# Working out a group's slots behind the third stage's statistics instead of in front of the first weighing

## The chip, the cores and the metric

One Trainium2 chip, one core. The metric is the device time of one execution in microseconds. In what follows PE is TensorE, DVE is VectorE, ACT is ScalarE, POOL is GpSimd and SP is SyncE.

## What is computed

64 graphs of 256 nodes with 256 features pass through two layers. Each of the four blocks is added to its input, which is first layer-normalised. The first is an attention over the graph's edges, the second a Mamba-2 block, the third a sum over four edge relations, and the fourth a mixture of eight experts to which each token is routed by its largest probability.

```
x = x + gnn_attention(_layernorm(x), adj, W, a)
x = x + mamba2_block(_layernorm(x), W_in, conv_w, ..., W_out, W_lin, b_lin)
x = x + relational_gnn(_layernorm(x), adj, weight, bias)
x = x + moe_ffn(_layernorm(x), gate_w, gate_b, w1, b1, w2, b2)
```

The routing is what the change is about:

```
C = max(1, math.ceil(CAPACITY_FACTOR * T / E))
idx = jnp.argmax(probs, axis=-1)
pos = (jnp.cumsum(one_hot, axis=0) * one_hot).sum(-1).astype(jnp.int32) - 1
kept = pos < C
buf = jnp.zeros((E, C, D), dtype=h.dtype).at[idx, pos_safe].set(x, mode='drop')
```

A token's slot is its expert's first row plus its place among that expert's tokens. Tokens beyond the capacity are not served.

## The kernel before

The program has two parts. The first runs over the 64 graphs (called batches) and holds all but the experts; it ends near 2420 us. The second runs the experts over 71 tiles of 256 tokens. Only the first part is touched.

The first part is a software pipeline written out by hand. `rounds` calls a function `step(b1_, b2_, b3_, turn_)` on every engine. In one step batch b1_ is in the first stage (attention), b2_, the batch before it, in the second (Mamba), and b3_, the one before that, in the third (relations and gate). The steps of an engine are executed in the order in which they are written; between engines there are only semaphores. Two batches form a group of 512 tokens, GB = 2, so steps alternate. In those with `turn_[1] == 0` the group before is routed (`best_expert`, with `counts` at the step's end), in those with `turn_[1] == 1` its slots are worked out (`slots`). The loop body holds two steps, one of each kind; the first six and the last few steps stand unrolled.

The order on DVE in one step (names as in the program):

- statistics of x of batch b1_ (`deviation(0, ...)`), xn2, then the convolution's taps, dt and the running sums cs, cs3, then the attention scores e and their maxima;
- g and xdt (L1023, L1027). PE needs them for the first exponents (L1256);
- in steps with slots: `slots` (L941 to L952), ten instructions on 4 or 32 numbers in a partition. It makes `slot` and `tid`, which POOL scatters one step later (`place`), and `prk`, the tokens' shares, which SP stores (L431);
- `weigh(range(0, 2))` (L901): the first two pairs of heads, once ACT's exponentials are there (L655);
- rsum and x1 (L1038, L1052), the attention's result. PE's next product with xT (`attend`, L1220) writes into the same two banks and so waits for x1_ready. Then the statistics of x1, from which POOL makes rstd and shift and ACT makes xn1, which PE turns (L1206);
- the other weighings, y (L1063, L1068), the third stage's result `row` (L1075). ACT squares y, POOL adds the squares up (y2h L561, y2s L564), and PE sums y2s over partitions (L1451, out_made);
- in steps with slots: the statistics of `row` (`deviation(3, ...)`, its last instruction L877). In steps with routing `best_expert` stands here and these statistics come after the mean square;
- the mean square, `ve[4]` (L1085). It waits for out_made; POOL raises it to the power -1/2 (L492), DVE makes x2 from it (L1094) and x2's statistics. PE needs x2_ready before the second pair of projections into bank 4 of the next step.

PE's order in a step: projections (L1211, L1281), masks by xp (L1328), relations (L1227, in pieces), transposes, attention's transposes (L1384), the first exponents (L1256 to L1265), a piece of relations, the attention product (L1411), the second exponents, a piece of relations, `attend` (L1220), the diagonal product (L1429), the last relations, xn1's transposes (L1206), the output projection (L1444), y2s (L1451).

Of the kernel before, what the change touches and what calls it, by code (L numbers as in the profile page):

```python
# [20 lines left out]
def need(eng, sem, n):  # L21

    if isinstance(n, int) and n <= 0:
        return
    eng.wait_ge(sem, n)
# [24 lines left out]
def graph_mamba_moe(nc, io, out):  # L50
# [39 lines left out]
    with ctx:  # L90
# [256 lines left out]
        def is_first(b):  # L347

            return isinstance(b, int) and b == 0
# [44 lines left out]
        def to_route(turn_):  # L394

            if turn_ is None or turn_[1] != 0 or is_first(turn_[0]):
                return None
            return turn_[0] - 1

        def to_slot(turn_):  # L400

            if turn_ is None or turn_[1] != 1 or is_first(turn_[0]):
                return None
            return turn_[0] - 1
# [390 lines left out]
        def _(dve):  # L795
# [73 lines left out]
            def deviation(i, src, chain, b):  # L869

                for t in range(T):
                    ins = v.bn_stats(stats[i][:, t, :], src[:, t, 0:D])
                chain.link(dve, ins, b, carry)
                for t in range(T):
                    ins = v.bn_aggr(mv[i][:, t, :], stats[i][:, t, :])
                chain.link(dve, ins, b)
                v.tensor_scalar(ve[i][:], mv[i][:, :, 1], EPS, None, ALU.add).then_inc(var_ready[i], 1)  # L877
# [27 lines left out]
            def best_expert(g):  # L905

                lk = lambda ins: chr_.link(dve, ins, g)
                three = lambda a: a[:].unsqueeze(2).broadcast_to([P, GT, E])
                chr_.start()
                dve.wait_ge(lg_in, GB * g + GB)  # L910
                lk(v.tensor_reduce(lmax[:], lg[:], AX.X, ALU.max))
                v.tensor_tensor(lg2[:], lg[:], three(lmax), ALU.subtract).then_inc(lg_ready, 1)
                dve.wait_ge(ge_ready, g + 1)
                v.tensor_reduce(gsum[:], ge[:], AX.X, ALU.add)
                lk(v.tensor_reduce(gmax[:], ge[:], AX.X, ALU.max))
                v.reciprocal(grec[:], gsum[:])
                lk(v.tensor_tensor(eq[:], ge[:], three(gmax), ALU.is_equal))
                v.tensor_tensor(prb[:], gmax[:], grec[:], ALU.mult)

                lk(v.tensor_tensor(rv[:], eq[:], rev[:], ALU.mult))  # L920
                lk(v.tensor_reduce(rmax[:], rv[:], AX.X, ALU.max))
                need(dve, cum_made, g)
                v.tensor_tensor(ohb[:], rev[:], three(rmax), ALU.is_equal).then_inc(oh_ready, 1)
                v.tensor_tensor(oh[:], rev[:], three(rmax), ALU.is_equal)
                need(dve, ids_out, 16 * GT * g)
                lk(v.tensor_scalar(tokf[:], tokf[:], float(GB * N), None, ALU.add))
                v.tensor_copy(tid[:], tokf[:])
                v.tensor_scalar(tr1[:], tokf[:], float(SLOTS + SPARE + 1), None, ALU.add)
# [9 lines left out]
            def slots(g):  # L938

                lk = lambda ins: chr_.link(dve, ins, g)  # L940
                v.tensor_tensor(limo[:], lim[:], oh[:], ALU.mult)  # L941
                lk(v.tensor_tensor(cumo[:], cum[:], oh[:], ALU.mult))
                v.tensor_reduce(lm[:], limo[:], AX.X, ALU.add)
                lk(v.tensor_reduce(slot1[:], cumo[:], AX.X, ALU.add))

                v.tensor_tensor(kept[:], slot1[:], lm[:], ALU.is_le)
                lk(v.tensor_tensor(df[:], slot1[:], tr1[:], ALU.subtract))
                lk(v.tensor_tensor(kd[:], kept[:], df[:], ALU.mult))
                lk(v.scalar_tensor_tensor(df[:], kd[:], -1.0, tr1[:], ALU.add, ALU.add))
                v.tensor_copy(slot[:], df[:]).then_inc(slot_ready, 1)  # L950
                need(dve, prk_out, 16 * g)
                v.tensor_tensor(prk[:, :, 0], prb[:], kept[:], ALU.mult).then_inc(prk_ready, 1)  # L952
# [5 lines left out]
            def step(b1_, b2_, b3_, turn_):  # L958
# [62 lines left out]
                if b2_ is not None:  # L1021
# [3 lines left out]
                    for t in range(T):  # L1025
# [2 lines left out]
                                              bank[4 + t][:, :].rearrange("p (h c) -> p h c", h=H),  # L1028
                                              dtT[:, t, :].unsqueeze(2).broadcast_to([P, H, HD]), ALU.mult)
                        ins.then_inc(xdt_ready, 1)  # L1030
                g_ = to_slot(turn_)
                if g_ is not None:
                    slots(g_)
                if b2_ is not None:
                    weigh(range(0, 2), b2_)
                if b1_ is not None:
# [40 lines left out]
                g_ = to_route(turn_)  # L1077
                if g_ is not None:
                    best_expert(g_)
                elif b3_ is not None:  # L1080
                    dve.wait_ge(x3_ready, b3_ + 1)
                    deviation(3, row[:, :, 0:D], ch4, b3_)
                if b2_ is not None:
                    dve.wait_ge(out_made, b2_ + 1)
                    v.tensor_scalar(ve[4][:], bank[5][:, 0:T], 1.0 / DIN, EPS, ALU.mult, ALU.add).then_inc(var_ready[4], 1)  # L1085
# [21 lines left out]
                if g_ is not None:  # L1107
                    counts(g_)

            rounds(dve, step)  # L1110
            best_expert(GROUPS - 1)
            counts(GROUPS - 1)
# [439 lines left out]
```

## Time and profile before

| | us |
|---|---|
| median of three runs | 3455.23 |
| lowest, highest | 3453.88, 3458.61 |
| profiled execution | 3474.3 |
| its span | 3472.6 |

| engine | busy us | share of the span |
|---|---|---|
| PE | 3346.5 | 96% |
| DVE | 2531.6 | 73% |
| ACT | 1745.4 | 50% |
| POOL | 1842.6 | 53% |

The span is what the trace covers of the profiled execution; the time of that execution is 1.7 us longer. It is to be compared with the median only with its own distance of 19 us in mind. The granted clock of TensorE was 0.986 of its full 2.4 GHz on average.

How to read it: a timeline row has the start in us from the span's start, the time taken in us, the engine, the line, the operation, output<-inputs and the number of instructions merged into the row; in brackets stands the idle time in front of it and what ended it. Matmuls are pipelined, so the rows of PE overlap a little, and a wait shorter than the pipeline is deep shows as a longer row rather than as idle time. A list of waits names the waiting line, what it waited for, the total in us, the number of times and the longest.

### The profile page before, as it was taken

The numbers are of one execution on the slowest core, as the hardware profiler recorded it, in microseconds if no ns is written. First come the engines' busy times: TensorE is split into PE (matmuls) and PEld (weight loads), VectorE is DVE, ScalarE is ACT, GpSimd is POOL, SyncE is SP. The second block draws the span as 40 slices with busy tenths as digits, with TensorE's granted clock in tenths as the row PEclk, the third lists the DMA queues.
The fourth block names the chain that finished last, engine by engine and source line by source line (L and its number), as shares of the span: only waits on it lengthen the run. The fifth ranks groups of instructions, "written<-read, shape, count | busy, mean of one in ns | idle before, by whom it ended". The sixth has DMA issues, their size and how long they took to land.

```text
span 3472.6 us, 60750 instructions
## 1 busy us (share of the span) xinstructions
PE 3346.5 (96%) x18826; PEld 2741.4 (79%) x18826; DVE 2531.6 (73%) x7305; ACT 1745.4 (50%) x3434; POOL 1842.6 (53%) x2172
## 2 busy tenths in 40 slices
PE   7999999999999999999999999996899999999998
PEld 6777777777777777777777777775788888888887
DVE  4888888878888888888888888886344444444444
ACT  3666656655656656656566565663223333333222
POOL 3455555555555565555655556554445555555543
PEclk8999999999999999999999999998899999999999
DMA  3111111111111111111111111110555555555553
GB/s 125 41 38 52 40 46 46 37 37 52 40 39 49 40 40 52 37 46 45 37 52 40 46 46 37 52 37 22 174 195 191 192 195 198 197 192 193 193 194 129
DMA packets 168166, 304.66 MB, mean 88 GB/s; under 512 B 38000, under 2 KB 140400, under 8 KB 149936
## 3 DMA queue, kind: packets, MB, share of 16 engines
q0 software_dynamic: 38272, 196.98, 16.5%
q1 hardware_dynamic: 92880, 72.41, 7.3%
q10 hardware_dynamic: 36960, 34.62, 3.3%
q8 instruction: 26, 0.43, 0.1%
q14 instruction: 28, 0.23, 0.0%
HBM read 250.77 MB, written 53.17 MB: 88 GB/s over the span
## 4 chain that ended last, share of the span: by engine, by line
PE 92%; DVE 3%; issue 2%; POOL 1%; another core or an unknown queue 1%; ACT 1%; DMA 1%; SPq 0%; DVEq 0%; ACTq 0%; POOLq 0%
PE bank L1211 14%; PE bank L1485 14%; PE bank L1499 14%; PE bank L1227 13%; PE bank L1328 7%; PE bank L1444 6%; PE bank L1429 5%; PE bank L1220 4%; PE bank L1411 3%; PE bank L1359 2%; PE bank L1281 2%; DVE decay L901 1%; PE bank L1350 1%; PE bank L1451 1%; PE bank L1474 1%
## 5 line engine op out<-in xcount | busy, mean ns | idle before, releaser
L786 ACT ACTIVATE decay<-bank,w_up 128x256 f32<-128x256 f32 x568 | 269.0, 474 | 700.0 <-PE bank L1485 694.2
L1227 PE MATMUL bank<-w_rel,hT 128*128 128x264 f32 x2048 | 540.7, 397 | 0.0
L1211 PE MATMUL bank<-xn1T,w_in 128*128 128x256 f32 x2304 | 524.1, 382 | 2.9 <-ACT xn1T L637 0.8
L1485 PE MATMUL bank<-zs,w_up 128*128 128x256 f32 x2272 | 503.8, 380 | 0.6 <-ACT zs L637 0.6
L1499 PE MATMUL bank<-w_dn,decay 128*128 128x256 f32 x2272 | 502.1, 379 | 0.0
L1211 PEld LDWEIGHTS bank<-xn1T,w_in 128*128 128x128 f32 x2304 | 433.1, 190 | 61.0 <-issue 1.5
L1485 PEld LDWEIGHTS bank<-zs,w_up 128*128 128x128 f32 x2272 | 432.9, 191 | 60.1 <-issue 0.9
L1499 PEld LDWEIGHTS bank<-w_dn,decay 128*128 128x128 f32 x2272 | 426.2, 190 | 55.1
L1159 DVE TENSOR_TENSOR hT<-bank,w_dn 128x256 f32<-128x256 f32 x142 | 60.3, 425 | 535.9 <-PE bank L1499 535.9
L892 DVE SCALAR_TENSOR_TENSOR conv<-bank,conv_w,conv 128x255 f32<-128x255 f32 (+2 forms) x960 | 426.2, 477 | 20.8
L1227 PEld LDWEIGHTS bank<-w_rel,hT 128*128 128x128 f32 x2048 | 358.6, 190 | 85.7 <-issue 32.8
L506 POOL TENSOR_SCALAR masks<-adjt_sb 128x512 fp32r<-128x512 int32 x256 | 419.4, 1651 | 5.4
L492 POOL TENSOR_TENSOR rstd<-ve,mhalf 128x2 f32<-128x2 f32 x256 | 212.9, 831 | 284.0 <-DVE ve L877 239.5
L369 POOL TENSOR_TENSOR beats<-mhalf 128x1 f32<-128x1 f32 x372 | 100.1, 269 | 462.7 <-DVE hT L1159 335.9
L901 DVE SCALAR_TENSOR_TENSOR decay<-decay,g 128x768 f32<-128x768 f32 x256 | 266.5, 1081 | 60.2 <-ACT decay L655 57.3
L543 POOL TENSOR_TENSOR x2b<-x,b_rel 128x264 f32<-128x264 f32 x128 | 93.9, 753 | 397.6 <-DVE xdt L1027 389.9
L1328 PE MATMUL bank<-masks,xp 128*128 128x512 f32 x1024 | 275.7, 414 | 5.7 <-ACT xp L637 5.7
L655 ACT ACTIVATE decay<-bank 128x768 f32<-128x768 f32 x256 | 193.6, 808 | 144.7 <-PE bank L1265 115.6
L1328 PEld LDWEIGHTS bank<-masks,xp 128*128 128x128 f32 x1024 | 189.1, 190 | 68.3 <-ACT hT L637 25.1
L1444 PE MATMUL bank<-w_proj,y 128*128 128x264 f32 x1024 | 239.4, 387 | 0.7 <-DVE y L1068 0.7
L1444 PEld LDWEIGHTS bank<-w_proj,y 128*128 128x128 f32 x1024 | 189.2, 190 | 31.2 <-DVE y L1068 2.3
L591 POOL DMA_INDIRECT w_in<-token_rows,idc x142 | 178.9, 1260 | 43.6 <-issue 43.6
(258 smaller groups left out, 5997.0 us busy)
## 6 DMA issues: line engine op xcount, KB each, us to landing
token_rows<-row SPq DMA_DIRECT2D x64, 266.0 KB, 3.0
xT_sb<-in_xT ACTq DMA_DIRECT2D x64, 256.0 KB
x_sb<-in_x ACTq DMA_DIRECT2D x64, 256.0 KB, 3.0
adj_sb<-in_adj SPq DMA_DIRECT2D x64, 256.0 KB, 3.4
adjt_sb<-in_adjT SPq DMA_DIRECT2D x64, 256.0 KB, 3.5
out<-row SPq DMA_DIRECT2D x64, 256.0 KB, 2.4
w_in<-token_rows,idc POOLq DMA_INDIRECT x142
out<-hT,ids POOLq DMA_INDIRECT x142
```

What stands on the lines that cost most here:

```text
L492: gp.tensor_tensor(rstd[i][:], ve[i][:], mhalf[:], ALU.pow).then_inc(rstd_ready[i], 1)
L506: ins = gp.tensor_scalar(masks[:, :, r, :], adjt[:], float(r + 1), None, ALU.is_equal)
L655: nc.scalar.activation(decay[:, 2 * j:2 * j + 2, :], expo_banks[j % 2][:, :, 0:TRI], ACT.Exp).then_inc(decay_ready, 1)
L786: nc.scalar.activation(hid(f), bank[f % 4][:, 0:GROUP], ACT.Relu, bias=b1[q % 2][:, f:f + 1]).then_inc(hid_ready, 1)
L892: ins = v.scalar_tensor_tensor(conv[:, c, k:N], src[:, 0:N - k], conv_w[:, c, TAPS - 1 - k:TAPS - k], conv[:, c, k:N], ALU.mult, ALU.add)
L901: v.scalar_tensor_tensor(decay[:, 2 * j:2 * j + 2, :], decay[:, 2 * j:2 * j + 2, :], 1.0, g[:, 0:TRI].unsqueeze(1).broadcast_to([P, 2, TRI ...
L1211: ins = mm(dst, w_in[:, k, first:first + P], xn1T[:, k, :], start=k == 0, stop=k == DK - 1)
L1227: ins = mm(bank[6 + t][:, 0:GX], hT[:, d, r * N + t * P:r * N + (t + 1) * P], w_rel[:, r, d, :], start=r == 0 and d == 0, stop=r == R - 1 ...
L1328: ins = mm(bank[6 + c][:, :], xp[part][:, t, d * P:(d + 1) * P], masks[:, t, 2 * c:2 * c + 2, :], start=t == 0 and part == 0, stop=t == T ...
L1444: ins = mm(bank[(4, 2)[t]][:, 0:GX], y[:, j, t * P:(t + 1) * P], w_proj[:, j, :], start=j == 0, stop=j == XB - 1)
L1485: ins = mm(bank[f % 4][:, 0:GROUP], w1[i][:, k, f * P:(f + 1) * P], xgT[:, k, :], start=k == 0, stop=k == DK - 1)
L1499: ins = mm(bank[4 + j][:, 0:D], hid(f)[:, j * P:(j + 1) * P], w2[i][:, f, :], start=f == 0, stop=f == FB - 1)
```

## The change

The call of `slots` in a step that has one is moved. It stood behind xdt and in front of the first weighing. Now it stands behind the statistics of `row` and in front of the wait for out_made and the mean square. A step without a second stage (b2_ is None; only the very last one) keeps the call where it was, and so does the call after the last step. The variable for the group is renamed, since `g_` is set anew in between. 30 calls are moved, those for groups 0 to 29.

```diff
--- before.py
+++ after.py
@@ -1028,9 +1028,9 @@
                                               bank[4 + t][:, :].rearrange("p (h c) -> p h c", h=H),
                                               dtT[:, t, :].unsqueeze(2).broadcast_to([P, H, HD]), ALU.mult)
                         ins.then_inc(xdt_ready, 1)
-                g_ = to_slot(turn_)
-                if g_ is not None:
-                    slots(g_)
+                placed = to_slot(turn_)
+                if placed is not None and b2_ is None:
+                    slots(placed)
                 if b2_ is not None:
                     weigh(range(0, 2), b2_)
                 if b1_ is not None:
@@ -1080,6 +1080,8 @@
                 elif b3_ is not None:
                     dve.wait_ge(x3_ready, b3_ + 1)
                     deviation(3, row[:, :, 0:D], ch4, b3_)
+                if placed is not None and b2_ is not None:
+                    slots(placed)
                 if b2_ is not None:
                     dve.wait_ge(out_made, b2_ + 1)
                     v.tensor_scalar(ve[4][:], bank[5][:, 0:T], 1.0 / DIN, EPS, ALU.mult, ALU.add).then_inc(var_ready[4], 1)
```

DVE, an unrolled step with slots, around the old place, before. The names in it: `decay<-decay,g` is a weighing, `x<-bank,rsum,x_sb` is x1.

```order
L1027 TENSOR_TENSOR xdt<-bank,g 128x512 x2
L941 TENSOR_TENSOR limo<-lim,oh 128x32
L942 TENSOR_TENSOR cumo<-cum,oh 128x32
L943 TENSOR_REDUCE lm<-limo 128x4
L944 TENSOR_REDUCE slot<-cumo 128x4
L946 TENSOR_TENSOR kept<-slot,lm 128x4
L947 TENSOR_TENSOR df<-slot,tr 128x4
L948 TENSOR_TENSOR kd<-kept,df 128x4
L949 SCALAR_TENSOR_TENSOR df<-kd,tr 128x4
L950 CAST slot<-df 128x4
L952 TENSOR_TENSOR prk<-prb,kept 128x4
L901 SCALAR_TENSOR_TENSOR decay<-decay,g 128x768 x2
```

The same place in the change:

```order
L1027 TENSOR_TENSOR xdt<-bank,g 128x512 x2
L901 SCALAR_TENSOR_TENSOR decay<-decay,g 128x768 x2
L1038 RECIPROCAL rsum<-esum 128x2
L1052 SCALAR_TENSOR_TENSOR x<-bank,rsum,x_sb 128x264 x2
L872 BN_STATS stats<-x 128x6 x2
```

The weighing and x1 follow xdt directly.

DVE, the end of the same step, before. `row<-bank,x2b` is the third stage's result, `ve<-row` its variance, `ve<-bank` the mean square, `x<-bank,rstd,x1b` is x2.

```order
L1075 TENSOR_TENSOR row<-bank,x2b 128x2x264
L872 BN_STATS stats<-row 128x6 x2
L371 MEMSET beats 128x1
L875 BN_AGGR row<-stats 128x2 x2
L877 TENSOR_SCALAR ve<-row 128x2
L1085 TENSOR_SCALAR ve<-bank 128x2
L1094 SCALAR_TENSOR_TENSOR x<-bank,rstd,x1b 128x264 x2
```

The same place in the change:

```order
L877 TENSOR_SCALAR ve<-row 128x2
L941 TENSOR_TENSOR limo<-lim,oh 128x32
L942 TENSOR_TENSOR cumo<-cum,oh 128x32
L943 TENSOR_REDUCE lm<-limo 128x4
L944 TENSOR_REDUCE slot<-cumo 128x4
L946 TENSOR_TENSOR kept<-slot,lm 128x4
L947 TENSOR_TENSOR df<-slot,tr 128x4
L948 TENSOR_TENSOR kd<-kept,df 128x4
L949 SCALAR_TENSOR_TENSOR df<-kd,tr 128x4
L950 CAST slot<-df 128x4
L952 TENSOR_TENSOR prk<-prb,kept 128x4
L1087 TENSOR_SCALAR ve<-bank 128x2
```

The ten instructions stand between the variance and the mean square. The lines behind the edit have numbers two higher. In the loop body they stand in the same way. The instructions of PE, ACT, POOL and SP and their order are the same as before.

## Rows read from the trace of the kernel before

**Rows 1.** The page's chain that ended last, shares of the span by engine
```profile
PE 92%; DVE 3%; issue 2%; POOL 1%; another core or an unknown queue 1%; ACT 1%; DMA 1%; SPq 0%; DVEq 0%; ACTq 0%; POOLq 0%
```

**Rows 2.** Waits of TensorE's matmuls, 150 to 2350 us: total us, times, longest
```profile
PE bank L1220 <- DVE x L1052: 34.6, 33, 6.7
...
PE bank L1206 <- ACT xn L754: 2.0, 1, 2.0
```

**Rows 3.** Timeline of TensorE, step with slots: start us, us, engine line
```profile
1157.62 0.61 PE L1451 MATMUL bank<-ones_row,y2s 128*128 128x1 f32 x4
...
1178.65 0.58 PE L1256 MATMUL bank<-cs,sel 32*128 32x256 bf16 x4
...
1184.76 2.09 PE L1220 MATMUL bank<-w_gc,xT_sb 128*128 128x274 f32 x8 [0.91 <-DVE x L1052]
...
1194.63 0.61 PE L1451 MATMUL bank<-ones_row,y2s 128*128 128x1 f32 x4
```

**Rows 4.** Timeline of TensorE, the next step, without slots
```profile
1215.51 0.36 PE L1256 MATMUL bank<-cs,sel 32*128 32x256 bf16 x4
...
1220.32 2.02 PE L1220 MATMUL bank<-w_gc,xT_sb 128*128 128x274 f32 x8
...
1226.01 0.60 PE L1206 MATMUL bank<-identf,xn 128*128 128x128 f32 x4
...
1230.11 0.61 PE L1451 MATMUL bank<-ones_row,y2s 128*128 128x1 f32 x4
```

**Rows 5.** Timeline of DVE, step with slots, around the slots
```profile
1177.61 1.29 DVE L1027 TENSOR_TENSOR xdt<-bank,g 128x512 f32<-128x512 f32 x2
...
1178.81 0.18 DVE L941 TENSOR_TENSOR limo<-lim,oh 128x32 f32<-128x32 f32 x1
...
1181.26 0.15 DVE L952 TENSOR_TENSOR prk<-prb,kept 128x4 f32<-128x4 f32 x1
...
1183.72 0.89 DVE L1052 SCALAR_TENSOR_TENSOR x<-bank,rsum,x_sb 128x264 f32<-128x264 f32 x2
```

**Rows 6.** Timeline of DVE, step without slots, the first weighing
```profile
1216.95 2.07 DVE L901 SCALAR_TENSOR_TENSOR decay<-decay,g 128x768 f32<-128x768 f32 x2 [1.42 <-ACT decay L655]
```

**Rows 7.** Timeline of DVE, end of the step with slots
```profile
1193.18 0.62 DVE L877 TENSOR_SCALAR ve<-row 128x2 f32<-128x2 f32 x1
...
1195.27 0.16 DVE L1085 TENSOR_SCALAR ve<-bank 128x2 f32<-128x2 f32 x1 [1.47 <-PE bank L1451]
```

**Rows 8.** Timeline of POOL, step with slots: masks, y2s, power
```profile
1180.72 4.41 POOL L506 TENSOR_SCALAR masks<-adjt_sb 128x512 fp32r<-128x512 int32 x3
...
1193.85 0.72 POOL L564 TENSOR_TENSOR y2s<-y2h 128x256 f32<-128x256 f32 x1
...
1194.53 0.71 POOL L492 TENSOR_TENSOR row<-ve,mhalf 128x2 f32<-128x2 f32 x1
```

**Rows 9.** Timeline of all engines, slots of the last group
```profile
2422.23 0.18 DVE L941 TENSOR_TENSOR limo<-lim,oh 128x32 f32<-128x32 f32 x1
...
2423.61 0.16 DVE L952 TENSOR_TENSOR prk<-prb,kept 128x4 f32<-128x4 f32 x1
```

**Rows 10.** Timelines of POOL and DVE in the routing, end of a step
```profile
1156.81 0.76 POOL L564 TENSOR_TENSOR y2s<-y2h 128x256 f32<-128x256 f32 x1
...
1156.89 0.72 DVE L920 TENSOR_TENSOR rv<-eq,rev 128x32 f32<-128x32 f32 x1
```

**Rows 11.** Timeline of DVE, xn2 after a step with routing, then after one with slots
```profile
1163.45 0.73 DVE L882 TENSOR_SCALAR xn<-x,mv,rstd 128x256 f32<-128x256 f32 x2
...
1199.90 0.73 DVE L882 TENSOR_SCALAR xn<-x,mv,rstd 128x256 f32<-128x256 f32 x2
```

**Rows 12.** Timeline of ScalarE, step without slots, xn1
```profile
1224.77 1.09 ACT L754 ACTIVATE xn<-x,shift,rstd 128x256 f32<-128x256 f32 x2 [3.81 <-POOL shift L554]
```

**Rows 13.** Timelines of SP's queue and of POOL after the step with slots
```profile
1196.94 0.39 SPq L436 DMA_DIRECT2D adj_sb<-in_adj  x1
...
1205.08 1.94 POOL L530 TENSOR_SCALAR noedge<-adj_sb 128x512 f32<-128x512 int32 x1
```

## The prediction

> **What bounds the kernel now.** I read the chain that ended last first. TensorE carries 92% of it [rows 1], so an edit on VectorE (DVE) counts only where TensorE waits for DVE. The list of waits comes next: between 150 and 2350 us the largest total of matmul waits is L1220 on x1 (L1052), 34.6 us in 33 waits [rows 2]; 29 of them are alike, the other four are single stalls, the longest of 6.7 us. Then I laid two neighbouring steps side by side on TensorE. A step is counted from one L1451 (the mean square's sums) to the next. A step that works out slots (call it odd) lasts 1194.63 - 1157.62 = 37.01 us [rows 3]; the step without them (even) 1230.11 - 1194.63 = 35.48 us [rows 3, 4]. The DVE timeline of the same two steps shows why.
>
> **Where the odd step loses.** In the odd step L1256 starts at +21.03 and takes 0.58 us, in the even one at +20.88 and takes 0.36 [rows 3, 4]. So 0.15 + 0.22 = 0.37 us is lost up to the first exponents. That part isn't the slots': DVE enters the odd step later, because the routing (best_expert) stood in the tail before it. Its xn2 (L882) starts at 1163.45, that is +5.83, against +5.27 in the even step [rows 11]. L1220 then starts at +27.14 against +25.69, 1.45 later. Take off the 0.37 and 1.08 us is left. 0.91 of it is the marked wait for x1 [rows 3], the rest is pipeline filling. This part is the slots': xdt ends at 1178.90, slots run from 1178.81 until 1181.41 and x1 comes at 1183.72 [rows 5]. In the even step DVE has nothing there and idles 1.42 us until the exponentials are ready [rows 6]. Slots of 2.60 us in a gap of 1.42 push the weighing back by about 1.2.
>
> **What the change takes away.** Ten DVE instructions leave this place in 30 odd steps (groups 0 to 29). 29 of them have an L1220; the thirtieth, near the end, starts no next batch, and I put it at 0. Each of the 29 can gain at most the 1.08, which is all that sets it apart from an even step there. **Gain: 29 x 1.08 = 31 us.**
>
> **What it adds.** The same ten instructions now stand between the third stage's variance (L877, ends 1193.18 + 0.62 = 1193.80) and the mean square (L1085 in before), which waits for TensorE's L1451 and starts at 1195.27 after 1.47 us of idle time [rows 7]. The cover is thus 1.5 us. What the slots need there is not shown by the trace of before, so bounds: run with GpSimd (POOL) silent, in the last group, they take 2423.61 + 0.16 - 2422.23 = 1.54 us [rows 9]. At the old place they take 2.60, the last part of it beside POOL's masks [rows 5, 8]. At the new place POOL first does the y2s sum (1193.85 to 1194.57), then a power (1194.53 to 1195.24) [rows 8]. How such an addition holds up a small DVE instruction is seen in the routing: L920, two operands in SBUF, takes 0.72 us beside a y2s that began 0.08 us before it [rows 10], where limo, of the same size, takes 0.18 alone [rows 9]. I expect limo to slip in, cumo to be held until y2s ends (0.6 more) and perhaps kept to brush the power (0.1). So T = 1.54 + 0.65, about 2.2 us. It is nearer to the upper row because the same kinds of POOL work run beside it, but only one or two instructions can be caught, not three.
>
> The slots start about 1193.73 (instructions without a dependence start some 0.08 before the former one's recorded end). With T = 1.54 the mean square starts where it does now, with 2.2 about 0.6 later, with 2.6 about 1.0 later. Everything behind it on DVE moves by the same d: the power on POOL that waits for it, x2, its statistics, the next batch's statistics, xn2, the taps, dt, cs3, xdt. DVE has next to no idle time on that way in an even step.
>
> **What the delay costs on TensorE.** x2 itself has room: bank 4 is needed after the first two blocks of projections. The price is paid some 20 us later, where the first exponents need xdt. The trace gives the exchange rate: in the odd step DVE is 0.56 late at xn2 and TensorE loses 0.37 by the first exponents [rows 3, 4, 11]. So about 0.2 is absorbed and the rest is passed on in full. With d = 0.6 an even step loses 0.4, with 0 nothing, with 1.0 it loses 0.8. After that DVE waits for the exponentials anyway and is in step again, so losses don't pile up. 29 even steps follow a moved group and start from it. **Loss: 29 x 0.4 = 12 us** (0 to 23).
>
> **Small things.** limo and cumo may in turn hold y2s up. y2s ends at 1194.57 and L1451 starts at 1194.63 [rows 3, 8], so TensorE has no room there, and y2s later by up to 0.2 us makes L1451 as late. But this and the lateness of DVE run in parallel, and the larger of the two counts, so it adds nothing to 0.4. slot and tid are read by POOL's scatter only in the next step: no cost. On SP's queue the store of the shares (L431) now waits for a prk that comes around 1195.9 us; behind it is queued the load of adj, issued at 1196.94, which has to be there before noedge at 1205.08 [rows 13]. Even 1 us later there are 7 us left: cost 0. TensorE's, ScalarE's, POOL's and SP's own orders are unchanged.
>
> A rule of the Trainium skill bears on T. The row first: prk has two operands in SBUF, starts at 1181.26, takes 0.15 us, and the first mask on POOL has been running since 1180.72, about 1.5 us each [rows 5, 8]. It was not held. The page "SBUF — State Buffer", section "Who interferes with whom", says that a DVE instruction with two SBUF inputs contends with a GpSimd instruction that reads SBUF, and that the one that starts second is blocked until the first ends. By that rule kept would wait for the whole power too, T would be about 2.3, and the time 3 us more than my forecast. The row of prk speaks against a full block each time, the row of L920 for it.
>
> **The sum.** -31 + 12 = -19 us. The profiled execution took 3474.3 us (span 3472.6), 19 above the median of 3455.2; the steps of a kind agree within 0.1 us apart from a few with single stalls, so I take the same difference for both: 3474.3 becomes 3455, and the median becomes **3436 us**.
>
> **Rivals.**
> (a) The slots fit in the gap (T up to 1.8): nothing is passed on, all of the gain stays, 3424 us. For it: the idle time there is 1.47 us and the bare work 1.54. Against: y2s runs right there.
> (b) The slots stay as long as they were (2.6): loss 23, the sum -8, 3447 us. For it: POOL is busy here as well. Against: its work ends at 1195.24, and the last four instructions have DVE to themselves.
> (c) **Another wait takes the place of x1's**, and the kernel gets slower. In the even step the weighing collides with POOL's masks; they end later, and with them the shift that xn1 needs: xn1 is done at 1224.77 + 1.09 = 1225.86, and L1206 needs it at 1226.01 [rows 4, 12]. The odd step will run like that, with 0.15 us of room. Each microsecond beyond it is lost at L1206 in full. With T = 2.2 the turning point is 0.7 beyond the room; with the masks 1.2 us later than in the even steps the sum is -19 + 35 = +16, 3471 us. Against it: over 60 steps L1206 waited for xn1 once, 2.0 us [rows 2].
> (d) The gain doesn't come, because x1 is held by something else as well (exponentials, the attention product), and only part of the loss remains: between -5 and +5, 3455 us. Against it: x1 in even steps is early enough.
>
> **Chances.** Forecast (T 1.9 to 2.4, 3430 to 3443) 55%; (a) 15%; (b) 13%; (d) 8%; (c) 9%. A measurement of this kernel can tell about 0.2% (7 us) from no change. The forecast, (a) and most of (b) lie beyond that: faster 77%. Within it: (d) and a part of (b), 13%. Slower: (c) and a remainder, 10%. The range of 8 in 10 reaches from 3423 to 3452.
>
> **What would show it.** In after: no wait of L1220 for x1 in odd steps and an odd step of 35.9 to 36.1 us (right), or a wait at L1206 in it (c). Slots at the new place of 2.2 us with cumo at 0.7 and the idle time before the mean square gone. Even steps of 35.9 rather than 35.5, with L1256 stretched and the start of xn2 0.6 later. Even steps unchanged mean (a), 36.3 and more (b). The forecast is wrong altogether if odd steps don't fall below 36.5.

## The result

The changed kernel takes 3423.22 us (3420.38 to 3426.49, four runs), the kernel before in the same runs 3454.56. The ratio is 0.9908, with an interval of 0.9896 to 0.9921: 32 us or 0.92% faster. The forecast was 3436 in a range of 3423 to 3452, so the way was right and the gain too small by 12 us; the measured time lies on the lower edge of the range. It is what rival (a) gave, 3424.

The chain that ended last, from the page of after, shares of the span by engine [rows 1]:

```profile
PE 94%; DVE 2%; issue 2%; POOL 1%; DMA 1%; ACT 0%; another core or an unknown queue 0%; SPq 0%; ACTq 0%; DVEq 0%; POOLq 0%
```

Waits of TensorE's matmuls from 150 to 2350 us: total, times, longest. L1222 is L1220 of before, L1208 is L1206 [rows 2]:

```profile
PE bank L1208 <- ACT xn L754: 2.7, 2, 2.0
PE bank L1222 <- DVE x L1052: 1.6, 2, 1.2
```

34.6 us of waiting for x1 have become 1.6; the two left are single stalls in even steps.

TensorE in two neighbouring steps of after: a step with slots from 1197.74 on, the next without from 1233.72 on. L1453, L1258, L1222 and L1208 answer to L1451, L1256, L1220 and L1206 [rows 3, 4]:

```profile
1197.74 0.61 PE L1453 MATMUL bank<-ones_row,y2s 128*128 128x1 f32 x4
...
1218.77 0.58 PE L1258 MATMUL bank<-cs,sel 32*128 32x256 bf16 x4
...
1223.81 2.02 PE L1222 MATMUL bank<-w_gc,xT_sb 128*128 128x274 f32 x8
...
1229.50 0.60 PE L1208 MATMUL bank<-identf,xn 128*128 128x128 f32 x4
...
1233.72 0.51 PE L1453 MATMUL bank<-ones_row,y2s 128*128 128x1 f32 x4
...
1254.52 0.35 PE L1258 MATMUL bank<-cs,sel 32*128 32x256 bf16 x4
...
1259.33 2.02 PE L1222 MATMUL bank<-w_gc,xT_sb 128*128 128x274 f32 x8
...
1269.16 0.61 PE L1453 MATMUL bank<-ones_row,y2s 128*128 128x1 f32 x4
```

The step with slots lasts 35.98 us instead of 37.01. L1222 starts in it at +26.07, before at +27.14: this is the 1.08 of the prediction, all but 0.01 of it. The step without slots lasts 35.44 instead of 35.48. Nothing of the expected 0.4 is in it: L1258 starts at +20.80 and takes 0.35. A pair is 1.07 us shorter, and 29 of these are 31 us.

DVE in the same step with slots, around the old place and then at the new one [rows 5 to 7, 9]:

```profile
1217.73 1.29 DVE L1027 TENSOR_TENSOR xdt<-bank,g 128x512 f32<-128x512 f32 x2
1220.44 1.96 DVE L901 SCALAR_TENSOR_TENSOR decay<-decay,g 128x768 f32<-128x768 f32 x2 [1.42 <-ACT decay L655]
...
1222.55 0.89 DVE L1052 SCALAR_TENSOR_TENSOR x<-bank,rsum,x_sb 128x264 f32<-128x264 f32 x2
...
1232.61 0.17 DVE L877 TENSOR_SCALAR ve<-row 128x2 f32<-128x2 f32 x1
1232.69 0.18 DVE L941 TENSOR_TENSOR limo<-lim,oh 128x32 f32<-128x32 f32 x1
1232.79 0.18 DVE L942 TENSOR_TENSOR cumo<-cum,oh 128x32 f32<-128x32 f32 x1
...
1233.32 0.26 DVE L946 TENSOR_TENSOR kept<-slot,lm 128x4 f32<-128x4 f32 x1
...
1233.69 0.16 DVE L948 TENSOR_TENSOR kd<-kept,df 128x4 f32<-128x4 f32 x1
...
1234.19 0.17 DVE L952 TENSOR_TENSOR prk<-prb,kept 128x4 f32<-128x4 f32 x1
1234.27 0.15 DVE L1087 TENSOR_SCALAR ve<-bank 128x2 f32<-128x2 f32 x1
...
1238.89 0.73 DVE L882 TENSOR_SCALAR xn<-x,mv,rstd 128x256 f32<-128x256 f32 x2
```

POOL beside it [rows 8]:

```profile
1221.55 5.41 POOL L506 TENSOR_SCALAR masks<-adjt_sb 128x512 fp32r<-128x512 int32 x3
...
1232.82 0.74 POOL L564 TENSOR_TENSOR y2s<-y2h 128x256 f32<-128x256 f32 x1
1233.52 0.72 POOL L492 TENSOR_TENSOR row<-ve,mhalf 128x2 f32<-128x2 f32 x1
```

At the old place the weighing waits 1.42 us for the exponentials, as in a step without slots, and x1 starts at +24.81, before at +26.10. At the new place the ten instructions take 1234.19 + 0.17 - 1232.69 = 1.67 us, 0.13 above the bare 1.54 and far from the 2.2 of the forecast; in all 29 odd steps of after that start a next batch they take 1.63 to 1.68. That they fit where DVE idled 1.47 us comes from the overlap at both ends: limo begins 0.09 before the recorded end of L877, and the mean square 0.09 before that of prk. The mean square starts at +0.55 here. (After has two kinds of steps with slots. In this one, 18 of the 29, a mask held DVE's y up and the sums' row at 1233.72 takes 0.51; in the other kind it takes 0.61 and starts 0.10 earlier, the mean square is at +0.65, and the next step lasts 35.51.) Before it was at +0.64. xn2 starts at +5.17, before at +5.27: DVE enters the next step no later than it did. But the gap is full: DVE no longer idles before the mean square.

The thirtieth moved call, in the step that starts no next batch, ran much as the forecast had it for all: limo slipped in, cumo (2305.45) took 0.71 us and ended 0.05 after POOL's additions y2h (2304.68 to 2306.11), and the ten took 2.32 us. They also began 0.6 to 0.7 us earlier before the sums than elsewhere, so the mean square still stood at +0.64.

The profiled executions differ by 51 us in span (3472.6 and 3421.2), more than the runs do. The steps explain 31; the rest are single stalls that the trace of before happened to hold, one of 6.7 us at L1220 among them [rows 2]. That is why the medians, not the two profiled executions, give the size of the gain.

### The profile page after: what moved, and what is told of

It reads as the page before. It is cut to its first block, busy times and chain, and to the rows that moved or that the text cites. A ratio compares the mean times of both kernels' runs of the same rounds, so it can differ in the third digit from the quotient of the medians.

```text
span 3421.2 us, 60750 instructions
## 1 busy us (share of the span) xinstructions
PE 3333.2 (97%) x18826; PEld 2738.9 (80%) x18826; DVE 2506.8 (73%) x7305; ACT 1745.0 (51%) x3434; POOL 1871.5 (55%) x2172
## 4 chain that ended last, share of the span: by engine, by line
PE 94%; DVE 2%; issue 2%; POOL 1%; DMA 1%; ACT 0%; another core or an unknown queue 0%; SPq 0%; ACTq 0%; DVEq 0%; POOLq 0%
PE bank L1213 14%; PE bank L1487 14%; PE bank L1501 14%; PE bank L1229 14%; PE bank L1330 7%; PE bank L1446 6%; PE bank L1431 5%; PE bank L1222 3%; PE bank L1413 3%; PE bank L1361 2%; PE bank L1283 2%; PE bank L1352 1%; PE bank L1258 1%; PE bank L1476 1%; PE bank L1453 1%
## 5 line engine op out<-in xcount | busy, mean ns | idle before, releaser
L506 POOL TENSOR_SCALAR masks<-adjt_sb 128x512 fp32r<-128x512 int32 x256 | 456.4, 1795 | 5.4
L369 POOL TENSOR_TENSOR beats<-mhalf 128x1 f32<-128x1 f32 x372 | 121.6, 327 | 462.5 <-DVE hT L1161 336.1
L492 POOL TENSOR_TENSOR rstd<-ve,mhalf 128x2 f32<-128x2 f32 x256 | 190.5, 744 | 251.0 <-DVE ve L877 206.7
```

The lines of the kernel that those rows point to most:

```text
L492: gp.tensor_tensor(rstd[i][:], ve[i][:], mhalf[:], ALU.pow).then_inc(rstd_ready[i], 1)
L506: ins = gp.tensor_scalar(masks[:, :, r, :], adjt[:], float(r + 1), None, ALU.is_equal)
```

## The experiments

**How late may the mean square be?** The forecast's loss was a rate (all but 0.2 us is passed on) times a lateness. The filler is a statistics instruction on DVE whose result nobody reads; it touches only `row` and a tile of its own. It goes once behind and once ahead of the slots.

```diff
+            def filler(n):
+                for i in range(n):
+                    v.bn_stats(pad[:, i, :], row[:, i % T, 0:D])
...
                 if placed is not None and b2_ is not None:
                     slots(placed)
+                    filler(1)
```

> The changed kernel plus one bn_stats of 128x256 on DVE (0.37 us of start-to-start time, result unused) between the moved slots and the mean square, in 30 steps. Theory A (the prediction's exchange rate: 0.2 us of lateness is absorbed, the rest is passed on): 29 x (0.37 - 0.2) = 5 us slower than the changed kernel, so 26 us under the kernel before. Theory B (DVE has far more room behind the mean square than the prediction said): no slower than the changed kernel, 31 us under the kernel before.

Measured: 3433.07 us, ratio 0.9928 (0.9912 to 0.9945), 7 us above the changed kernel by the ratios. The intervals of the two overlap, so the step itself has to show it. DVE and TensorE of this run (L1093 is the mean square, L1459 the sums):

```profile
1161.78 0.42 DVE L957 BATCH_NORM_STATS2 pad<-row 128x6 f32<-128x256 f32 x1
1162.12 0.14 DVE L1093 TENSOR_SCALAR ve<-bank 128x2 f32<-128x2 f32 x1
...
1166.72 0.73 DVE L883 TENSOR_SCALAR xn<-x,mv,rstd 128x256 f32<-128x256 f32 x2
```

```profile
1161.13 0.61 PE L1459 MATMUL bank<-ones_row,y2s 128*128 128x1 f32 x4
...
1182.01 0.65 PE L1264 MATMUL bank<-cs,sel 32*128 32x256 bf16 x4
...
1196.95 0.61 PE L1459 MATMUL bank<-ones_row,y2s 128*128 128x1 f32 x4
```

The sums' row is of the kind with 0.61. The mean square starts at +0.99, 0.34 later than in such a step of after, and xn2 at +5.59. L1264 takes 0.65 instead of 0.35, and the step lasts 35.82 instead of 35.51. So 0.34 us of lateness costs TensorE 0.31 in this step, and xn2, at +5.28 in such a step of after, is 0.31 later too. Theory A holds, B falls: DVE has no room behind the mean square, and even less is absorbed than the 0.2 assumed.

The same filler ahead of the slots:

```diff
                 if placed is not None and b2_ is not None:
+                    filler(1)
                     slots(placed)
```

> The same filler, but in front of the moved slots, so that limo and cumo come while POOL's y2s is running. Theory A (the hold-up the prediction counted on is real and was only missed because both additions slipped in before y2s began): limo is held until y2s ends, slots take 2.0 to 2.2 us instead of 1.66, the mean square is 0.65 to 0.75 late, 29 x 0.5 = 14 us slower than the changed kernel, 17 us under before. Theory B (small additions are not held by y2s at this place at all): the same as the filler behind the slots, 26 us under before.

Measured: 3439.40 us, ratio 0.9951 (0.9934 to 0.9967), 15 us above the changed kernel; theory A said 14. DVE, then POOL (y2s is L565, the power L493, limo L942):

```profile
1160.97 0.57 DVE L942 TENSOR_TENSOR limo<-lim,oh 128x32 f32<-128x32 f32 x1
...
1162.80 0.17 DVE L953 TENSOR_TENSOR prk<-prb,kept 128x4 f32<-128x4 f32 x1
1162.88 0.15 DVE L1093 TENSOR_SCALAR ve<-bank 128x2 f32<-128x2 f32 x1
```

```profile
1160.77 0.72 POOL L565 TENSOR_TENSOR y2s<-y2h 128x256 f32<-128x256 f32 x1
1161.45 0.71 POOL L493 TENSOR_TENSOR row<-ve,mhalf 128x2 f32<-128x2 f32 x1
```

The mean square is at +1.22 against +0.55, since this sums' row (1161.66) is of the kind with 0.51: 0.67 late. limo, which takes 0.18 alone, takes 0.57 and ends at 1161.54, when y2s has ended at 1161.49. The slots now take 2.00 us. TensorE's step lasts 36.06 instead of 35.44. This is the hold-up that the forecast counted on. It is real, but the instruction has to begin while y2s runs. Without the filler limo and cumo have both started before y2s does (1232.69 and 1232.79 against 1232.82), and the next two instructions, the reductions lm (1233.01) and slot (1233.11), take 0.19 and 0.17 us beside it, as in the last group with POOL silent.

**A lateness of 1.1 us, first with three fillers.**

```diff
                     slots(placed)
+                    filler(3)
```

> Three fillers behind the moved slots: the mean square 1.12 us late, about as late as slots of 2.6 us would make it. Theory A (exchange rate): 29 x 0.92 = 27 us slower than the changed kernel, 4 us under before. Theory B (more room): at most 10 us slower than the changed kernel, 21 us or more under before.

Measured: 3575.33 us, ratio 1.0341 (1.0324 to 1.0359). Neither theory: 3.4% slower than before, 150 us above the changed kernel. The same happened with six fillers at the old place:

```diff
                 placed = to_slot(turn_)
                 if placed is not None and b2_ is None:
                     slots(placed)
+                elif placed is not None:
+                    filler(6)
```

> The changed kernel plus six fillers (2.24 us) at the old place, behind xdt and in front of the first weighing, where DVE now idles 1.42 us. Theory A (what cost time there was the length beyond the gap): the weighing starts 0.8 us late, x1 has 0.2 to 0.3 us of room, so 29 x 0.55 = 16 us slower than the changed kernel, 15 us under before, with a wait of L1222 for x1. Theory B (the cost came from the slots' collisions with POOL, which bn_stats doesn't have): no slower than the changed kernel.

Measured: 3560.31 us, ratio 1.0291 (1.0274 to 1.0309). Waits of DVE in the run with three, total, times and longest, and its timeline at the head of a loop round:

```profile
DVE stats L873 <- issue: 112.4, 27, 4.8
```

```profile
1006.74 0.75 DVE L873 BATCH_NORM_STATS2 stats<-x_sb 128x6 f32<-128x256 f32 x2 [3.76 <-issue]
```

DVE stands still for 4 us at the first instruction of each loop round, and nothing in the trace releases it. The page's list of queues, after and then the run with three fillers:

```profile
q14 instruction: 28, 0.23, 0.0%
```

```profile
q14 instruction: 163, 1.34, 0.1%
```

135 more instruction packets, 5 for each of 27 rounds. TensorE then waits 99.8 us in 27 waits for DVE's convolution taps in the run with three, and its mean granted clock is 0.971 there, 0.988 in after. Not counting those that only wait for a semaphore, DVE's loop body has 265 instructions in the changed kernel, 266 with one filler, 268 with three and 271 with six. So three short memsets, which hardly add time, were put in the fillers' place:

```diff
+                for i in range(n):
+                    v.memset(pad[:, i, 0:1], 0.0)
...
                     slots(placed)
+                    filler(3)
```

> The changed kernel plus three memsets of one column (0.06 to 0.1 us each) behind the moved slots. Theory A (the jump of the runs with three and six fillers comes from the number of DVE instructions: the loop body no longer lies where it can be run without being loaded again): 110 to 140 us slower than the changed kernel, DVE idle about 4 us at the head of the loop in each of 28 rounds, and some 130 more instruction packets. Theory B (the jump came from the fillers' length): at most 8 us slower than the changed kernel.

Measured: 3561.26 us, ratio 1.0297 (1.0280 to 1.0315), 134 us above the changed kernel. Its waits; the queue again has 163 packets:

```profile
DVE stats L873 <- issue: 129.7, 27, 5.3
```

Theory A's numbers hold: what the fillers do and how long they take doesn't make the jump, the instructions added do. The Trainium skill, "Runtime: NRT & Kernel Launch", section "Instruction fetch mechanics", gives a mechanism: most engines hold 512 instructions, filled in blocks of 256, and a branch taken to an instruction outside these two blocks has to load its block first. The packets and the idle time at the loop's head agree with that. The bound itself was not tested; the runs show only that 266 in this place don't jump and 268 do. Nor was the length of the loop parted from its place: the fillers also stand in an unrolled step ahead of it, so that the loop begins later by as many instructions.

So the two questions were asked again with one long instruction each:

```diff
+                v.tensor_reduce(pad[:, 0, 0:XB], w_proj[:], AX.X, ALU.add)
```

> The changed kernel plus ONE long instruction (a reduction of 128x1056, 1.1 us, result unused) between the moved slots and the mean square. It replaces the run with three short fillers, which cost 142 us over the changed kernel and had DVE idle 4.2 us once per loop round without a releaser. Theory A (the first two fillers' rate: all of the lateness but 0.05 us is passed on): 29 x 1.05 = 30 us slower than the changed kernel, within 3 us of the kernel before, and no idle DVE time at the loop's start. Theory A' (the prediction's rate, 0.2 absorbed): 26 us slower than the changed kernel. Theory B (a late mean square by 1.1 us itself sets off something worth 5 us a round): 140 us slower again.

Measured: 3455.40 us, ratio 0.9994 (0.9985 to 1.0004), 30 us above the changed kernel, as theory A said (30), and close to A' (26). The mean square (L1092) and TensorE's step:

```profile
1174.88 1.25 DVE L956 TENSOR_REDUCE pad<-w_proj 128x4 f32<-128x1056 f32 x1
1176.04 0.15 DVE L1092 TENSOR_SCALAR ve<-bank 128x2 f32<-128x2 f32 x1
```

```profile
1174.23 0.61 PE L1458 MATMUL bank<-ones_row,y2s 128*128 128x1 f32 x4
...
1195.91 0.68 PE L1263 MATMUL bank<-cs,sel 32*128 32x256 bf16 x4
...
1210.87 0.61 PE L1458 MATMUL bank<-ones_row,y2s 128*128 128x1 f32 x4
```

The mean square is at +1.81, 1.16 later than in a step of this kind of after, and the step lasts 36.64 instead of 35.51. DVE has no idle time at the loop's head, so theory B falls. With a late mean square of this size nearly the whole gain of the change is gone.

For the old place:

```diff
+                v.tensor_reduce(pad[:].rearrange("p a b -> p (a b)")[:, 0:R * DK], w_rel[:].rearrange("p r k o -> p (r k) o"), AX.X, ALU.add)
...
+                elif placed is not None:
+                    filler(1)
```

> The changed kernel plus ONE long instruction (a reduction of 128x2112, 2.2 us) at the old place, between xdt and the first weighing. Theory A (length beyond the 1.42 us gap): weighing 0.8 us late, 0.2 to 0.3 us of room at x1, 29 x 0.55 = 16 us slower than the changed kernel, 15 us under before, with a wait for x1 of 0.5 us in odd steps. Theory B (the slots' collisions with POOL made the loss, length does not count): no slower than the changed kernel.

Measured: 3440.57 us, ratio 0.9953 (0.9936 to 0.9969), 16 us above the changed kernel; theory A said 16. The wait for x1 is back:

```profile
PE bank L1228 <- DVE x L1058: 9.7, 31, 0.6
```

In the step at hand the filler puts the weighing about 0.8 us behind the gap's end, and odd steps last 36.41 us where those of after of the same kind last 35.87. So length beyond the gap costs there, less some 0.2 of room, also without a collision with POOL. That doesn't clear POOL of the old loss. Bare, the slots are 1.54 us long and would nearly fit the gap; what made them 2.60 stands in the trace of before, DVE and then POOL:

```profile
1179.45 0.47 DVE L946 TENSOR_TENSOR kept<-slot,lm 128x4 f32<-128x4 f32 x1
...
1180.02 0.60 DVE L948 TENSOR_TENSOR kd<-kept,df 128x4 f32<-128x4 f32 x1
...
1180.86 0.49 DVE L950 CAST slot<-df 128x4 int32<-128x4 f32 x1
```

```profile
1179.15 1.45 POOL L543 TENSOR_TENSOR x2b<-x,b_rel 128x264 f32<-128x264 f32 x2 [8.73 <-DVE xdt L1027]
```

In the last group, with POOL silent, these three take 0.16, 0.16 and 0.17. kd ends 0.02 after POOL's additions x2b, which xdt releases just as it lets the slots begin; the cast runs beside the first mask. The 1.06 us between 1.54 and 2.60 stand in these three. So at both places the collisions with POOL decide whether the slots fit, and beyond the gap every tenth counts. That the slots without collisions would have cost nothing at the old place is an estimate from these rows; no run shows it.

**A part of the slots back at the old place.**

```diff
+                elif placed is not None:
+                    slots_a(placed)
...
                 if placed is not None and b2_ is not None:
-                    slots(placed)
+                    slots_b(placed)
```

Here `slots_a` has limo, cumo, lm and slot, `slots_b` the other six.

> The changed kernel with the first four of the ten instructions (limo, cumo, lm, slot: 0.6 us) back at the old place and the other six at the new one. Theory A (a place costs only what exceeds its gap, 1.42 us at the old one): no wait for x1, the same time as the changed kernel within 3 us; the mean square is no earlier, since it waits for TensorE. Theory B (any DVE work ahead of the weighing costs): 29 x 0.6 = 17 us slower than the changed kernel.

Measured: 3428.36 us, ratio 0.9904 (0.9887 to 0.9920); the changed kernel run beside it 0.9906 (below). No difference. DVE at the old place, then at the new one:

```profile
1220.32 0.18 DVE L941 TENSOR_TENSOR limo<-lim,oh 128x32 f32<-128x32 f32 x1
...
1221.82 1.97 DVE L901 SCALAR_TENSOR_TENSOR decay<-decay,g 128x768 f32<-128x768 f32 x2 [0.91 <-ACT decay L655]
...
1234.33 0.61 DVE L951 TENSOR_TENSOR kd<-kept,df 128x4 f32<-128x4 f32 x1
...
1235.64 0.16 DVE L1096 TENSOR_SCALAR ve<-bank 128x2 f32<-128x2 f32 x1 [0.20 <-PE bank L1462]
```

The four hide in the gap (0.91 us of it are left). At the new place kd is now the one that begins during y2s (1234.20 to 1234.92) and takes 0.61 instead of 0.16, and the mean square waits 0.20 us for its sums again. It was hidden both ways.

**Using the gap that the change left.** A step with slots still loses 0.37 us up to the first exponents, since the routing in the tail before it makes DVE late. The routing's last four instructions aren't needed until the slots, so they can go into the gap behind xdt. They become a function of their own, `tokens`, which no longer runs with `best_expert`.

```diff
+            def tokens(g):
...
                 v.tensor_tensor(oh[:], rev[:], three(rmax), ALU.is_equal)
                 need(dve, ids_out, 16 * GT * g)
...
                 placed = to_slot(turn_)
+                if placed is not None:
+                    tokens(placed)
```

> The changed kernel, with the last four instructions of the routing (oh, tokf, tid, tr1: 0.45 us) taken out of the tail of the step with routing and put into the next step behind xdt, where DVE idles 1.42 us since the change. Nothing before the slots reads them. Theory A (the 0.37 us that a step with slots still loses up to the first exponents is DVE's lateness from the routing, passed on nearly one to one): 0.35 us less in each of 30 steps, 10 us faster than the changed kernel, 41 us under before, odd steps of 35.6 us. Theory B (those 0.37 us belong to something else): the same as the changed kernel, 31 us under before. Theory C (the gap is not free, the weighing gets late again): slower than the changed kernel.

Measured: 3420.03 us, ratio 0.9893 (0.9877 to 0.9910), 5 us under the changed kernel by the ratios, half of theory A. DVE in the step's head and behind xdt (L1094 is the mean square):

```profile
1196.43 0.16 DVE L1094 TENSOR_SCALAR ve<-bank 128x2 f32<-128x2 f32 x1 [0.20 <-PE bank L1461]
...
1201.47 0.73 DVE L882 TENSOR_SCALAR xn<-x,mv,rstd 128x256 f32<-128x256 f32 x2
...
1217.20 0.74 DVE L933 TENSOR_SCALAR tr<-tokf 128x4 f32<-128x4 f32 x1
1218.34 1.97 DVE L901 SCALAR_TENSOR_TENSOR decay<-decay,g 128x768 f32<-128x768 f32 x2 [0.40 <-ACT decay L655]
```

TensorE's sums begin at 1195.79 here. Of the 0.45 us taken away, 0.20 has turned into a wait of the mean square for them: it is at +0.64 instead of +0.81, and xn2 at +5.68 rather than +5.83. The step is 0.16 shorter (35.82), so what DVE does gain TensorE gains. That new wait is what theory A missed. In the gap tr1 (1217.20) is held up by POOL's x2b, which began at 1217.17 (0.74 instead of 0.16), and 0.40 us are still idle, so theory C falls. Since 5 us is little more than the intervals, it was run again with the changed kernel beside it:

> The changed kernel once more, beside the two below: 0.9908 of the kernel before, 31 to 32 us under it.

> The kernel with the routing's last four instructions behind xdt once more, in more rounds. Its first profile showed pairs of steps 0.16 us shorter than the changed kernel's, because DVE now waits 0.20 us for the mean square's sums in the step with routing. Theory: 30 x 0.16 = 5 us faster than the changed kernel in the same call. If the first result was noise: no difference.

Measured: the changed kernel 3429.79 us, ratio 0.9906 (0.9889 to 0.9922); this version 3422.85 us, ratio 0.9886 (0.9870 to 0.9903). Side by side it is 7 us faster, 3417.99 to 3423.94 against 3428.59 to 3430.27, four runs each and no overlap. It is the fastest version of this study, 1.1% under the kernel before.

## Why the prediction was right or wrong

- **What bounds the kernel, and the gain.** Right. 29 x 1.08 = 31 us were forecast, L1220 comes 1.07 earlier in the odd step, and nothing else held x1 there, so rival (d) falls. long2_old shows from the other side that length beyond the gap costs. The prediction took the slots' 2.60 us at the old place as partly due to the masks; most of what was above 1.54 came beside x2b, as the rows at long2_old show.
- **The duration T at the new place.** Wrong, and this is the step that failed: T = 1.54 + 0.65, about 2.2 us, forecast, 1.67 measured. The forecast let limo slip in and had cumo held until y2s ends, 0.6 more. cumo begins 0.10 us behind limo and y2s 0.13 us behind limo, so both slipped in, and cumo took its bare 0.18. With T = 1.67 the mean square isn't late, and the whole term 29 x 0.4 = 12 us falls away. What was added is 0.10 at kept (0.26 instead of 0.16): not by the power, as the forecast had it, but by y2s, for kept begins at 1233.32 and ends at 1233.58, 0.02 after y2s. kd begins at 1233.69 while the power runs from 1233.52 to 1234.24, and takes its bare 0.16. The hold-up itself exists: fill1_ahead brings it out at limo, split at kd, and the thirtieth call at cumo.
- **The rate.** Too mild. Taken from odd against even steps it was "all but 0.2". For 0.34, 0.67 and 1.16 us of lateness of the mean square (fill1_behind, fill1_ahead, long1_behind) the step shown lasts 0.31, 0.62 and 1.13 longer: all but 0.03 to 0.05. The medians, 7, 15 and 30 us over the changed kernel, give 0.24, 0.51 and 1.02 in each of 29 steps, but their intervals of some 5 us are 0.2 a step wide and can't tell the two apart. With the forecast lateness of 0.6 the loss would have been nearly 0.6 a step rather than 0.4, so an error in the other direction stood beside the first. It didn't matter, since the lateness was 0. Why odd against even steps showed a milder rate was not tried.
- **The small things.** y2s starts at 1232.82, right behind the start of cumo and 0.08 behind the end of y2h (1232.74), as before; it takes 0.74 instead of 0.72. The load of adj behind the store of the shares is issued at 1235.94, that is +2.22, before at +2.31: the later shares hold nothing up.
- **Rival (c), the masks.** The masks did end later, as described. The three masks take 5.41 us instead of 4.41 [rows 8]. ACT's row for xn1 in the same step of after:

```profile
1228.17 1.09 ACT L754 ACTIVATE xn<-x,shift,rstd 128x256 f32<-128x256 f32 x2 [3.71 <-POOL shift L554]
```

It ends at 1229.26 and L1208 starts at 1229.50: the room was enough, 0.24 us.
- **The choice between the cases.** (a) had 15% because its T had to be under 1.8 with y2s running. The bare time was 1.54 and the gap 1.47, and whether cumo is caught hung on hundredths of a microsecond: the prediction had the slots start at 1193.73 and y2s at 1193.85, and with the 0.10 by which cumo follows limo its start is 1193.83, ahead of y2s. Its own rows spoke for (a). It came so in all 29 steps, and in the one shown by 0.03 us (cumo 1232.79, y2s 1232.82), so 15% was too little. The prices also don't quite fit together: by the prediction's own d and rate, T of 1.9 to 2.4 gives 3427 to 3441, not 3430 to 3443.

The rule weighed in the prediction, that a DVE instruction with two SBUF inputs and a GpSimd instruction that reads SBUF shut each other out (the Trainium skill, "SBUF — State Buffer", section "Who interferes with whom"), fits limo in fill1_ahead (held until 0.05 us after y2s ends) and kept in after (until 0.02 after it). It does not fit kd beside the power, which wasn't held at all. By that rule the prediction put T at 2.3; it was 1.67, and the measurement decides.

## What to carry to other kernels

Before moving work of an engine into a gap, compare its bare length with the gap, and then look what the other engine runs beside it and when that starts, to the tenth of a microsecond: limo and cumo, begun just before POOL's addition, cost nothing extra, and begun 0.3 us later they cost 0.3. At the old place the same ten instructions grew from 1.54 to 2.60 us beside POOL. A delay on a side engine that has no idle time until its next delivery is passed on nearly one to one, here 20 us later. And look for new idle time at a loop's head after adding instructions to its body: three memsets that hardly take time cost 4 to 5 us a round here.

## What the runs showed of the hardware

- Three more DVE instructions in a loop of 265 (semaphore waits not counted), and three in an unrolled step ahead of it, cost 134 us as bare memsets and 150 us as statistics instructions; 130 and 112 us of it stand as idle time at the loop's head, with 135 more instruction packets each. One more cost nothing of the kind.
- A small DVE instruction that is held by POOL's addition ends 0.02 to 0.05 us after it (kept in after, limo in fill1_ahead), but beside a two-column power on POOL (0.72 us) kd isn't held. Why was not tried.
- DVE's small reductions with one input (lm, slot) take 0.19 and 0.17 us beside the same addition that holds limo for 0.39.
